# Local attention written out over its elements, with the weight blocks turned by transposing transfers

## What is computed

```python
def attn(x):                                  # x: layernorm(h)
    q, k, v = split(x @ w_qkv + b_qkv); q, k = rope(q), rope(k)
    out_local = masked_softmax(qb @ kb.T * scale, causal) @ vb          # inside blocks of 64
    lm = softmax(pool_q @ kb.T * scale) @ vb                            # 4 landmarks per block
    ...                                                                 # attention over landmarks
    return ((1 - gate) * out_local + gate * out_global) @ w_out + b_out
def ffn(x):
    return linear(silu(linear(x, w_gate)) * linear(x, w_up), w_down)    # linear(x, w): q_act(x) @ q_w(w).T
```

## Time and profile before

| | |
|---|---|
| median of 3 runs | 1832.39 us |
| profiled execution | 1829.61 us, span 1827.8 us, mean TensorE clock 0.867 |
| tokenizer and load of constants | about 0 to 235 us |
| local attention | about 235 to 908 us |
| the other attention stages | about 908 to 1430 us |
| feed-forward | about 1430 to 1828 us |
| TensorE, VectorE, ScalarE, GpSimd busy in the span | 85%, 73%, 57%, 30% |
| DMA queues | one of data: 154 MB, 26% of 16 engines; two of instructions: 33 and 27 packets |

### The profile page before, as it was taken

The page is one execution under the profiler, slowest core; times in us unless marked ns, Lnnn a source line. Parts: engine busy times, 40 slices in busy tenths (PEclk is TensorE's granted clock), DMA queues, the critical chain, the costliest instruction groups (busy, mean ns, idle before and its releaser), DMA issues. The chain is left out here.

```text
span 1827.8 us, 35108 instructions
## 1 busy us (share of the span) xinstructions
PE 1548.6 (85%) x11908; PEld 1069.0 (58%) x12006; DVE 1327.4 (73%) x2446; ACT 1040.8 (57%) x2579; POOL 539.7 (30%) x583
## 2 busy tenths in 40 slices
PE   2177749999999999999677896598988499999998
PEld 2177626676676677667456685465656244444543
DVE  8999746777777777777324362388887489999997
ACT  7799527887888887887412241366665233333332
POOL 0000014544544554444200000044444233333332
PEclk8555569999999999999786656799998799999999
DMA  2022252222223222222220363344454101111111
GB/s 58 2 61 61 61 172 86 75 75 99 87 75 106 85 75 99 75 87 90 76 85 0 127 207 110 117 148 148 151 157 129 46 29 46 46 46 46 46 46 52
DMA packets 122044, 154.77 MB, mean 85 GB/s; under 512 B 52480, under 2 KB 54144, under 8 KB 121984
## 3 DMA queue, kind: packets, MB, share of 16 engines
q1 hardware_dynamic: 121984, 154.01, 26.1%
HBM read 94.21 MB, written 59.77 MB: 84 GB/s over the span
## 5 line engine op out<-in xcount | busy, mean ns | idle before, releaser
L1057 PE MATMUL al_ps<-al_w,al_xT 128*128 128x512 f32 (+2 forms) x1024 | 350.9, 496 | 0.0
L1057 PEld LDWEIGHTS al_ps<-al_w,al_xT 128*128 128x128 f32 x1024 | 191.8, 192 | 127.0 <-issue 107.5
L2125 ACT ACTIVATE ff_zT<-ff_psz 128x1024 bf16<-128x1024 bf16 x64 | 65.5, 1024 | 239.4 <-PE ff_psz L2216 239.4
L2144 POOL TENSOR_TENSOR ff_zq<-ff_z,ff_back 128x1024 bf16<-128x1024 fp8e4 x64 | 122.2, 1909 | 252.0 <-DVE ff_z L2173 252.0
L442 PE MATMUL tk_ps<-tk_w,tk_l 128*128 128x64 f32 x512 | 113.0, 422 | 79.5 <-DVE tk_w L411 52.4
L442 PEld LDWEIGHTS tk_ps<-tk_w,tk_l 128*128 128x128 f32 x512 | 110.4, 332 | 82.1 <-issue 82.1
L739 POOL TENSOR_TENSOR al_qv<-al_qv,al_qe 128x512 f32<-128x512 f32 x48 | 62.0, 1291 | 248.2 <-PE al_ps L1130 248.2
L2224 PE MATMUL ff_acc<-wdT,ff_zT 128*128 128x512 bf16 x512 | 123.0, 384 | 2.2 <-ACT ff_zT L2125 2.2
L2199 PE MATMUL ff_gate<-wgT,xqT 128*128 128x512 bf16 x496 | 121.5, 383 | 3.8 <-ACTq L107 3.0
L2199 PE MATMUL ff_up<-wuT,xqT 128*128 128x512 bf16 x481 | 120.6, 383 | 1.6
L993 DVE TENSOR_REDUCE al_mx<-al_ps 128x32 f32<-128x2048 f32 x32 | 73.3, 2292 | 58.1 <-PE al_ps L1130 58.1
(11 more groups left out here) (308 smaller groups left out, 3520.0 us busy)
## 6 DMA issues: line engine op xcount, KB each, us to landing
al_hx<-h_s SPq DMA_DIRECT2D x36, 256.0 KB, 2.8
o_s<-al_o SPq DMA_DIRECT2D x32, 272.0 KB, 2.1
h_s<-tk_w SPq DMA_DIRECT2D x16, 512.0 KB, 3.8
v_s<-al_v SPq DMA_DIRECT2D x32, 256.0 KB, 2.1
k_s<-al_kT SPq DMA_DIRECT2D x32, 256.0 KB, 2.4
q_s<-al_qT SPq DMA_DIRECT2D x32, 256.0 KB, 2.6
lt_kT<-k_s SPq DMA_DIRECT2D x16, 512.0 KB, 4.6
lt_v<-v_s SPq DMA_DIRECT2D x16, 512.0 KB, 3.7
```

What stands on the lines that cost most here:

```text
L1057: ins = pe.matmul(out, xT[:, T, k], w[:, k, cols], start=False, stop=True, skip_group_check=True)
L2144: pool.tensor_tensor(zq[:, u].rearrange("p (k s) -> p k s", s=QB), z8[:, u].rearrange("p (k s) -> p k s", s=QB), back[:, u, :, None].to_br ...
```

## The change

All five lists of local attention are written out over the 16 elements; no hardware loop is left in the stage. The three blocks of weights, now all bf16 in one tile `qq`, are turned by `dma_start_transpose` on SyncE's queue straight into `wgT`, `wuT` and `wdT`. The transfers of u = 0 and 1 are issued behind the even tile's store of o, that of u = 2 behind the odd tile's, each after a wait for GpSimd's result (`wq_r`). GpSimd waits for the landing of the last element's transfer (`wt_in`) in place of `wt_p`. The transposes on TensorE, the copies on ScalarE, their semaphores and the waits for them go. In the diff the four other `Fori` lines change as the one that is shown.

```diff
-        qg, qu, qd = sb("qg", [P, D], BF16), sb("qu", [P, D]), sb("qd", [P, D], BF16)
-        qq = (qg, qu, qd)
+        qq = sb("qq", [P, 3, D], BF16)
...
-        wq_r, wt_p, wt_r = count("wq", 3), count("wtp", 3), count("wtr", 3)
+        wq_r = count("wq", 3)
+        wt_in = [count(f"wt_in{u}", 16) for u in range(3)]
...
                     sp.wait_ge(o_r.sem, o_r.upto(t))
                     sp.dma_start(row(o_s), o[:, T]).then_inc(o_out[T].sem, 16)
-
-            with sp.Fori(0, BATCH - 1) as i:
+                    for u in (range(2), range(2, 3))[T]:
+                        sp.wait_ge(wq_r.sem, wq_r.upto(i, u + 1))
+                        sp.dma_start_transpose(weight_targets(i)[u], qq[:, u]).then_inc(wt_in[u].sem, 16)
+
+            for i in range(BATCH - 1):
                 element(i)
             element(BATCH - 1, True)
...
-            sp.wait_ge(wq_in.sem, wq_in.upto(BATCH - 1))
+            for q in (wq_in, *wt_in):
+                sp.wait_ge(q.sem, q.upto(BATCH - 1))
...
-                    pool.wait_ge(wt_p.sem, wt_p.upto(n - 1, u + 1))
-                    pool.tensor_tensor(blocks(qq[u][:]), blocks(qv[:, u]), spread(qback[:, 16 * u:16 * u + 16]),
+                    pool.wait_ge(wt_in[u].sem, wt_in[u].done(n, 1))
+                    pool.tensor_tensor(blocks(qq[:, u]), blocks(qv[:, u]), spread(qback[:, 16 * u:16 * u + 16]),
...
-            def weights_out(i, u, bank):
-
-                act.wait_ge(wt_p.sem, wt_p.upto(i, u + 1))
-                act.activation(weight_targets(i)[u], (ps[:, bank] if u == 1 else half_bank(bank)).rearrange(
-                    "p (k r) -> p k r", k=KC), ACT.Copy
-                               ).then_inc(wt_r.sem, 1)
...
-                    if T == 1:
-                        weights_out(i, 1, 4)
...
-                        if T == 0:
-                            act.wait_ge(qT_r.sem, qT_r.upto(t))
-                        else:
-                            act.wait_ge(wt_r.sem, wt_r.upto(i, 2))
+                        act.wait_ge(qT_r.sem, qT_r.upto(t))
...
-                    weights_out(i, 2 * T, 6)
...
-            def weights(i, u, bank):
-
-                pe.wait_ge(wq_r.sem, wq_r.upto(i, u + 1))
-                for k in range(KC):
-                    if u == 1:
-                        ins = turned_in(ps[:, bank, k * P:(k + 1) * P], qu[:, k * P:(k + 1) * P], k)
-                    else:
-                        ins = pe.transpose(half_bank(bank)[:, k * P:(k + 1) * P], qq[u][:, k * P:(k + 1) * P],
-                                           K.identb[:])
-                ins.then_inc(wt_p.sem, 1)
...
-                    if T == 1:
-                        weights(i, 1, 4)
-
...
-                    pe.wait_ge(wt_r.sem, wt_r.upto(i, 1) if T else wt_r.done(i, 1))
...
-                    if not last:
-                        pe.wait_ge(xT_r.sem, xT_r.upto(t + 2))
-                    weights(i, 2 * T, 6)
```

More of the change, by code:

```diff
@@ L633, in weight_targets @@
                     K.wdT[:, bass.ds((n // 4) * KC, KC), bass.ds((n % 4) * P, P)])
-        def half_bank(bank):
-            return ps[:, bank, 0:D // 2].bitcast(BF16)
         blocks = lambda x: x.rearrange("p (k s) -> p k s", s=QB)
@@ L665, in tokens @@
                              ).then_inc(hx_in[T].sem, 16)
-            wq_in.credit(sp)
+            for q in (wq_in, *wt_in):
+                q.credit(sp)
             def weights(n):
@@ L760, in element @@
                 ls.end()
-            with pool.Fori(0, BATCH - 1) as i:
+            for i in range(BATCH - 1):
                 element(i)
@@ L767, in _ @@
         def _(act):
-            for q in (xn_r, xT_r, vs_r, v_r, tg_r, qT_r, kT_r, kbd_r, exp_r, pt_a, wt_r, bk_r, bq_r, bv_r):
+            for q in (xn_r, xT_r, vs_r, v_r, tg_r, qT_r, kT_r, kbd_r, exp_r, pt_a, bk_r, bq_r, bv_r):
                 q.credit(act)
@@ L895, in element @@
                         value_bias()
-            with act.Fori(0, BATCH - 1) as i:
+            for i in range(BATCH - 1):
                 element(i)
@@ L1031, in element @@
                     ls.end()
-            with dve.Fori(0, BATCH - 1) as i:
+            for i in range(BATCH - 1):
                 element(i)
@@ L1038, in _ @@
         def _(pe):
-            for q in (xt_p, vg_a, vg_b, k_p, q_p, qT_p, kT_p, s_p, pt_p, pv_p, wt_p):
+            for q in (xt_p, vg_a, vg_b, k_p, q_p, qT_p, kT_p, s_p, pt_p, pv_p):
                 q.credit(pe)
@@ L1167, in element @@
                     ins.then_inc(pv_p.sem, 1)
-            with pe.Fori(0, BATCH - 1) as i:
+            for i in range(BATCH - 1):
                 element(i)
```

## The result

The changed kernel takes 1811.97 us in the median of 4 runs (1811.07 to 1813.23), the kernel before 1832.28 beside it (4 runs, 1829.31 to 1834.97). The ratio is 0.989, 95% interval 0.9873 to 0.9907: faster by some 20 us. The profiled execution of the changed kernel took 1813.23 us with a span of 1811.4, against 1829.61 and 1827.8, so the two traces explain 16.4 us. The traced execution of before lies 2.7 us under the median of its runs, that of after 1.3 over its own, and that is the difference between 20.3 and 16.4.

A forecast was written before the change was run, and what follows sets the result against it. The prediction took TensorE to bound local attention: 1.32 us per element over fifteen elements (19.8) plus 1.6 for the last gave 21.4, less 2.6 for the tail, 18.8 us; 1832.4 - 18.8 = 1813.6 us, range 1806 to 1829.

The forecast's parts named there:

- What bounds the stage: Local attention: TensorE, busy 397.89 of 400 us, sets the time; work taken from ScalarE alone is worth nothing.
- Up weights: Odd tile, between pooled scores and masks: removing four float32 transposes frees 0.48 us of TensorE per element.
- Gate and down weights: Ahead of the product with V: removing each group of transposes frees 0.42 us of TensorE, lower bound 0.32.
- The last element: Local attention's already written-out last element: removing its transposes gives 1.6 us together, part at the lower clock.
- The tail: Stage end: the last transposing transfer lands behind the last output store, delaying the next stage by 2.6 us (0 to 8).
- tau: One transposing transfer's time on SyncE's queue and rings: 0.4 us issue, 4.3 to land; bounds 0.4 and 8, hidden to 9.3.
- Writing out: Sixteen loop bodies instead of two on all engines: about 50 more instruction packets, 0 to 5.6 us lost, counted as 0.
- dear transposes: Local attention: tau above 9.3 us makes the store of v late, holding ScalarE, then TensorE; kernel slower, chance 0.14.
- 2 tau - 18.6: Lateness of each local attention element in us if transposing transfers delay the store of v; slower from tau about 10.
- Fetch: Written-out local attention: 50 instruction blocks stalling TensorE 0.35 us each take 17.5 us, result 1831; chance 0.09.
- Rival 3: Local attention: ScalarE or VectorE comes last at once, only the odd tile's 0.48 us passes; 5.6 us, 1826.8; chance 0.05.
- The estimate of 5.2 us per block of weights: Transposing transfer by the skill's 1309 ns per 128x128 block: four take 5.2 us, under 9.3, with a 5.2 us tail.

The follow-up runs named there:

- e4: Changed kernel with the up weights' four float32 transposes back on TensorE and their copy on ScalarE: 1820.93 us, ratio 0.9969 to the kernel before.
- e5: Changed kernel with six more transposing transfers per element into a spare tile, eight ahead of the store of v: 1813.87 us, ratio 0.99 to the kernel before.
- e8: Changed kernel with two transposing transfers per feed-forward unit replacing TensorE's eight transposes and ScalarE's copy: 1808.28 us, ratio 0.9884 to the kernel before.
- e11: e8 with each unit's product with the down weights issued one unit later on TensorE: 1806.45 us, ratio 0.988 to the kernel before.
- e1: Changed kernel with only SyncE's list written out, the other four engines in the hardware loop: 1810.57 us, ratio 0.9929 to the kernel before.
- e2: Kernel before with all five lists written out, transposes still on TensorE: 1829.07 us, ratio 1.0017 to the kernel before.
- e9: Changed kernel measured once more, on one chip with the kernel before: 1813.76 us, ratio 0.9919.
- e10: Changed kernel with only SyncE's list written out, measured once more on the same chip as e9: 1809.4 us, ratio 0.9907 to the kernel before.
- e6: Changed kernel with fourteen more transposing transfers per element, sixteen ahead of the store of v: 1878.88 us, ratio 1.0263 to the kernel before.
- e3: Kernel before with the four bf16 transposes of gate and of down each done twice on TensorE: 1834.86 us, ratio 1.0034 to the kernel before.

## Why the prediction came out right

The forecast was 18.8 us from the median; 20.3 came at first, and 14.5 (1828.26 to 1813.76) when the change was measured again. The mechanism is the forecast's; that the total came so near is in part luck, as the end of this list shows. Its terms, one by one:

- **What bounds the stage** held. What is taken from TensorE is the kernel's gain, in every tile, and the ScalarE slack was enough: the tiles shrink by the 0.48 and 0.22 of TensorE's groups and by nothing for the three copies. One reading was off, to the safe side: without copy and wait ScalarE's two biases end 1.24 us earlier by the even tile's rows (1.39 us from the value copy's start to their end, 2.63 in the odd tile), not 1.04.
- **Up weights, 0.48 per element**: exact, by the tiles and by e4. The estimate came from two tiles that differ in nothing else.
- **Gate and down weights, 0.42 each**: over-sized; 0.22 each. This is the term that was mis-sized. I read the distance from one group's first weight load to the next group's, and took all of it as the group's own. About 0.2 of it is the step into the product with V, which its next neighbour inherits. Even the lower bound, the loads' own 0.32, was too high, since the neighbour's loads moved apart where the group's had been. So an element gave 0.93 in place of 1.32, and fifteen 13.9 instead of 19.8.
- **The last element, 1.6**: 3.78 was measured. 0.70 of it is the even tile (17.55 to 16.85). In the odd tile 0.42 is the change, by e4, e5, e8 and e11, whose last tile has 16.72 or 16.73. So the change itself gives 1.12. The other 2.66 us are TensorE's clock (last section), which the forecast didn't have.
- **The tail, 2.6**: 0.85. The landing was over-sized: 2.5 us after the transfer's start, not 4.3. The issue was under-sized, 1.24 us of SyncE and not 0.4, but it doesn't enter: a landing counts from the start, and what comes on top is only 887.77 - 887.41 = 0.36 by which the transfer starts behind the store, near the 0.4 by luck. With 2.5 - 2.2 (the store's own landing in this trace) this is 0.7 of the 0.85.
- **tau**: bounds 0.4 and 8 us; it is 1.2 to 1.3 us on SyncE (medians 1.23, 1.26 and 1.24 for the three blocks) and 2.4 to 2.5 from start to landing, far below the 9.3. Single ones took up to 2.6 on SyncE. Other transfers land a little later, v after 2.3 us where it was 2.1.
- **Writing out, 0**: held within the scatter, by e1, e2, e9 and e10. Packets rose by 46 in the larger queue, forecast about 50, without a wait.
- **The rivals**: dear transposes didn't come, but its chain is real and decides between 8 and 16 transfers. Its formula, 2 tau - 18.6, gives 16 x 1.25 - 18.6 = 1.4 us per element at e6, and with the 22.45 us that its sixteen took in the mean 3.8; 3.97 was measured. The closeness is partly luck, since the formula leaves out the 0.8 us that ScalarE absorbs. Fetch cost nothing in the stage. Rival 3, another engine last, isn't seen here, but in the feed-forward stage it is what stopped e8 and e11.

The errors, put together: 18.8 - 5.9 (gate and down in the loop, over-sized) - 0.5 (the same in the last element) + 1.8 (the tail, too dear) + 2.7 (the clock of the last tile, not foreseen) - 0.5 (start and rest of the kernel) = 16.4. The two over-sized terms had opposite signs, and the clock came on top by luck; without it the trace would show 13.7.

The Trainium skill (VectorE: DVE Perf Modes, The three transpose paths) has 390 ns for a 128x128 bf16 transpose on TensorE. This case's trace has less: four more cost 0.225 us in e3, 0.225 / 4 = 0.056 us each in a row between other work. For the crossbar the same section of the Trainium skill has 1309 ns per 128x128 block; here a transfer of four such blocks takes 1.25 us of SyncE and lands 2.5 us after its start, and fourteen in a row take 1.43 each. The estimate of 5.2 us per block of weights was four times the queue's time and twice the landing.

Between looped and written-out lists no tile differs, in e1 and after and in before and e2. The rule of the Trainium skill (Runtime: NRT & Kernel Launch, Instruction fetch mechanics) is on a taken branch whose target lies outside the fetched window, and the loop fetched nothing: its 460 us have no instruction packet. So no run here shows that the rule's case came up, and the equal tiles don't speak against it.

## What to carry to other kernels

To price work that is to be taken off a bound engine, compare a stretch that has it with one that lacks it, or double it: here this gave 0.48 and 0.23 us, and taking the groups away gave 0.48 and 0.22. The distance to the next group's start holds a step that stays behind. A transfer on a queue that is mostly empty is free until the first store behind it holds up a buffer, so find that buffer and its slack before asking what the transfer costs. And before moving work off the busiest engine, add up the serial chain of the next one: 99% against 92% busy was a lead of 0.05 us in 5.6.

## What was not expected of the hardware

**TensorE's clock in the last tile.** The same list of instructions takes 14.06 us in after and 16.73 in e8. In both TensorE stood idle for 4.1 us for VectorE, and the granted clock then fell to 0.50 (1.2 GHz). After, then e8, from there to the product with V:

```profile
878.66 0.47 PE L510 MATMUL al_ps<-cst,ap_pa 128*128 128x128 f32 x1 [4.11 <-DVE ap_pa L505]
...
882.70 1.00 PE L522 MATMUL al_ps<-ap_pT,al_v 128*128 128x64 f32 x8
883.77 2.06 PE L1134 MATMUL al_ps<-al_vbd,al_pT 128*64 128x34 f32 x64
```

```profile
877.66 0.33 PE L510 MATMUL al_ps<-cst,ap_pa 128*128 128x128 f32 x1 [4.10 <-DVE ap_pa L505]
...
882.12 1.81 PE L522 MATMUL al_ps<-ap_pT,al_v 128*128 128x64 f32 x8
883.85 3.63 PE L1134 MATMUL al_ps<-al_vbd,al_pT 128*64 128x34 f32 x64
```

Busy time and granted clock by stretch of 3 us (PE alone), after and then e8:

```profile
877.00:880.00 3.00, 1.34 (x7) 0.68 0.26 97
880.00:883.00 3.00, 2.46 (x16) 0.75 0.00 0
883.00:886.00 3.00, 2.76 (x71) 1.00 0.00 0
```

```profile
877.00:880.00 3.00, 2.34 (x11) 0.66 0.02 8
880.00:883.00 3.00, 2.47 (x13) 0.50 0.00 0
883.00:886.00 3.00, 3.00 (x45) 0.50 0.00 0
```

In after the clock is back at 1.00 (2.4 GHz) before the pooled sums, in e8 it stays at 0.50 to the stage's end, and that is 1.6 us in the product with V alone. It came back in both traces of the changed kernel (after and e9) and in both with SyncE's list alone written out (e1 and e10), 14.06 or 14.07 us each. It stayed low in e4, e5, e8 and e11, one trace each, and in the three kernels that turn gate and down on TensorE, before, e2 and e3. Why it rises in one and not in the other stays open. The local attention of e8 and e11 is that of after, list by list, so the change's instructions alone don't bring it. Nor does any trace show that it would come without the change. The 2.66 us in the difference of the two traces are therefore not shown to be a gain of the transfers.

**Transposing transfers in numbers.** 128 x 512 bf16, SBUF to SBUF: 544 packets; 1.23 to 1.26 us of SyncE in the median, up to 2.6; 2.4 to 2.5 us to landing in the median, at most 4.5 in after among the store and load traffic of this stage (6.3 in e6).
